# The scan's input in two PSUM banks, and seven other users in six: a decoder layer on one core

## The chip, the core and the metric

The kernel runs on one core of a Trainium2 chip. The metric is device time in microseconds: before the change 532.35 us, the median of 3 runs (530.22 to 536.63). The profile comes from one more execution, whose span is 528.4 us.

The core's engines run their own instruction streams and meet at semaphores: TensorE (PE; PEld is its weight load), VectorE (DVE), ScalarE (ACT), GpSimd (POOL) and SyncE (SP, which here issues DMAs). On-chip data lie in SBUF, or in PSUM, which has eight banks of 128 x 512 f32 that TensorE writes and that VectorE and ScalarE read and write.

## The reference

A decoder layer over 16 sequences of 128 tokens, width 128: a selective state-space scan with a mixture of 4 experts, attention to a context of 64 channels, and a second mixture of 8 experts with capacity. The change is in the first part:

```python
delta = jax.nn.softplus(jnp.einsum('bld,de->ble', x, Wd) + bd)
Bm = jnp.einsum('bld,ds->bls', x, WB) + bB
Cm = jnp.einsum('bld,ds->bls', x, WC) + bC
A = -jnp.exp(A_log)
def step(h, inps):
    x_t, d_t, B_t, C_t = inps
    bar_A = jnp.exp(jnp.minimum(d_t[:, :, None] * A, 2.0))
    bar_B = jnp.clip(d_t[:, :, None] * B_t[:, None, :], -2.0, 2.0)
    h = jnp.clip(bar_A * h + bar_B * x_t[:, :, None], -100.0, 100.0)
    y = jnp.sum(h * C_t[:, None, :], axis=-1) + x_t * D_param
    return (h, y)
...
hid = jax.nn.silu(jnp.einsum('nd,edf->enf', flat, up_w) + up_b[:, None, :])
all_out = jnp.einsum('enf,efd->end', hid, down_w) + down_b[:, None, :]
```

The state has 16 channels. The scan of one channel over time is one VectorE instruction on 128 x 512 elements (the model's width by four sequences).

## The kernel before, in words

**Tiles and units.** The 2048 tokens are four groups of 512 (`GW`). A unit is one state channel of one group: 64 units, 16 in a group. A loop over slots k, from -16 to past 64, is written out on every engine in the same order; slot k holds the work around unit k. A semaphore for each kind of result ties the streams. Nothing is scheduled at run time: each engine goes through its list in order, and a waiting instruction holds all behind it.

**One slot of the scan.** TensorE broadcasts a row B into bank 0 and a row C into bank 1 (`broadcast_row`, L1144). VectorE does `drive(k+1)` (L408: `bu = u * B`), `scan(k)` (L421: `h = a * h + bu` over time), `read_out(k-1)` (L456: `hc = h * C`) and then `around(k)`, a list of other work. GpSimd adds hc into yD (L871) when L456 is done. ScalarE makes the factors a by Exp, four units at once in each fourth slot (L970, `decay`), at least four slots ahead.

**TensorE's slot k** is `around(k)`, then `send_B(k+3)`, which waits until VectorE has read B of k+2, then `next_up(k+1)`, then `send_C(k+1)`, which waits until VectorE has done L456 of k. `up` (L1152) is one of the 16 up-projections of a group's mixture (4 experts by 4 tiles of 128); one is issued in a slot, from slot 16(g+1) on, so group g's mixture runs beside the scan of group g+1. ScalarE turns each into `hid` by a Silu (L983, `silu`), which is the last thing in its slot; TensorE's down-projections (L1161) read hid.

**The prologue** of group g+1 lies in the slots of group g's scan (that of group 0 ahead of all scans). Counted within a group's 16 slots: 2, turn xn (L1129) and copy it to xT on ScalarE (L961); 3, z = Wd x (L1172), B and C for all tokens (L1177), and on ScalarE Abs and Relu of z (L1029, L1032); 4, VectorE adds the bias to B and C and splits them in three bf16 parts (L356 to L366), ScalarE Exp and Ln; 5, transpose the parts (L1184) and copy them as `rows` (L1038); 6, the row of bounds (L1189), which VectorE reads in slot 12 (L375); 14, L1194, read in slot 15. Group 0's slots 7 to 14 also hold the transposes of fc1 (L1199), each copied out by ScalarE (L1045). The keys and values of attention are made in slots 10, 14 and 15 (`KV_SLOTS`).

**PSUM banks before:** 0 B, 1 C, 2 mixture (and z, keys, values), 3 and 4 up-projections in turn, 5 down-projections, 6 prologue, 7 attention. `claim(bank, reader)` makes TensorE wait for the last reader of the bank before it writes there again.

## Time and profile before

| what | before |
|---|---|
| median of 3 runs | 532.35 us (530.22 to 536.63) |
| span of the profiled execution | 528.4 us |
| PE, PEld busy | 342.2, 231.9 us |
| DVE busy | 354.0 us, 67% |
| ACT, POOL busy | 232.4, 225.2 us |
| the 64 scans L421 | 97.9 us busy, mean 1530 ns |
| the 64 adds L871 on POOL | 83.6 us busy, mean 1307 ns |
| DVE's waits for PE at L408 and L512 | 3.4 and 16.7 us |
| PE's waits for ACT at L1152 | 1.3 us in 2 places |

The page gives, for each line and kind of instruction, its busy time and the idle time of its engine just before it. A stretch of the timeline gives instructions in order of their start; brackets at a row's end hold how long its engine had been idle and what ended that. On TensorE one f32 product shows as two MATMUL rows merged to x2. The scan's loop lies between 25 and 302 us.

### The profile page before, as it was taken

What the parts mean: (1) busy time and instruction counts of PE and PEld (TensorE: products, weight loads), DVE (VectorE), ACT (ScalarE), POOL (GpSimd) and SP (SyncE); (2) the same over time, 40 slices, a digit from 0 to 9 for tenths busy, and PEclk for the clock granted to TensorE, in tenths of its full rate; (3) what the DMA queues carried; (4) which work ended last, traced back from release to release, by engine and by line L of the source; (5) the groups of instructions that cost most, each with busy time, mean ns of one, the idle gap of its engine ahead of it and who ended that gap; (6) DMA issues with size and microseconds to landing.
All of it is one profiled execution on the core that took longest, in us unless ns stands there. A gap on an engine that the chain in (4) does not pass through costs nothing.

```text
span 528.4 us, 5886 instructions
## 1 busy us (share of the span) xinstructions
PE 342.2 (65%) x1697; PEld 231.9 (44%) x1697; DVE 354.0 (67%) x977; ACT 232.4 (44%) x396; POOL 225.2 (43%) x214
## 2 busy tenths in 40 slices
PE   3216553859887769786795999873520799999200
PEld 2003231427544435463563667562310588898200
DVE  2579997996979999979999848557452012111085
ACT  2805533196643953575441385630200663553060
POOL 3313743436433345534334813342525035546354
PEclk9999999978989998989978999996555799999555
DMA  3999100000000000000000000010101311200152
GB/s 61 310 244 339 48 2 1 0 0 2 0 2 1 0 1 1 2 2 1 0 1 11 30 1 1 21 61 0 41 1 43 92 51 48 85 29 22 57 146 60
DMA packets 29464, 24.01 MB, mean 45 GB/s; under 512 B 5430, under 2 KB 23925, under 8 KB 29424
## 3 DMA queue, kind: packets, MB, share of 16 engines
q1 hardware_dynamic: 27032, 19.49, 13.4%
q0 software_dynamic: 2304, 4.04, 2.3%
q8 instruction: 14, 0.23, 0.2%
q14 instruction: 26, 0.21, 0.1%
q10 hardware_dynamic: 88, 0.03, 0.0%
HBM read 13.73 MB, written 10.52 MB: 46 GB/s over the span
## 4 chain that ended last, share of the span: by engine, by line
DVE 37%; PE 35%; issue 14%; ACT 5%; POOL 5%; DMA 3%; DVEq 1%; SPq 0%; ACTq 0%; POOLq 0%; another core or an unknown queue 0%
DVE h L421 9%; PE bank L1356 7%; PE bank L1345 6%; PE bank L1152 5%; PE bank L1161 5%; DVE hc L456 4%; PE bank L1144 3%; DVE stats L305 3%; DVE xrow L318 2%; DVE bu L408 2%; DVE acc L512 2%; DVE acc L328 2%; DVE mv L308 1%; DVE z L385 1%; DMA xT<-y_rows 1%
## 5 line engine op out<-in xcount | busy, mean ns | idle before, releaser
L871 POOL TENSOR_TENSOR yD<-yD,hc 128x512 f32<-128x512 f32 x64 | 83.6, 1307 | 138.4 <-DVE hc L456 118.5
L1144 PE MATMUL bank<-rows,selid 99*128 99x512 bf16 x128 | 61.7, 485 | 80.7 <-DVE bu L408 48.4
L421 DVE TENSOR_TENSOR_SCAN h<-a,bu 128x512 f32<-128x512 f32 x64 | 97.9, 1530 | 0.0
L1152 PE MATMUL bank<-yD,w 128*128 128x512 f32 x128 | 73.4, 658 | 1.7 <-ACT hid L983 1.3
L1161 PE MATMUL bank<-w,hid 128*128 128x128 f32 x512 | 73.3, 289 | 0.9 <-DVE lg L539 0.5
L1161 PEld LDWEIGHTS bank<-w,hid 128*128 128x128 f32 x512 | 67.2, 201 | 11.4 <-issue 8.9
L1144 PEld LDWEIGHTS bank<-rows,selid 99*128 99x128 bf16 x128 | 13.6, 108 | 132.5 <-DVE hc L456 70.6
L926 POOL DMA_INDIRECT y_rows<-yslot,dest x40 | 38.9, 973 | 52.5 <-DVE yslot L712 44.9
L712 DVE TENSOR_TENSOR yslot<-bank,w 128x128 f32<-128x128 f32 x40 | 11.6, 292 | 69.1 <-PE bank L1356 64.8
L983 ACT ACTIVATE hid<-bank,cols 128x512 f32<-128x512 f32 x64 | 43.7, 684 | 31.5 <-PE bank L1152 17.3
L408 DVE TENSOR_TENSOR bu<-u,bank 128x512 f32<-128x512 f32 x64 | 43.6, 682 | 18.7 <-issue 14.9
L1095 ACT ACTIVATE hid<-bank,cols 128x320 f32<-128x320 f32 x64 | 33.4, 527 | 29.5 <-PE bank L1345 25.5
L855 POOL TENSOR_TENSOR rstd<-vpe,nhalf 128x4 f32<-128x4 f32 x20 | 20.5, 1025 | 58.3 <-DVE vpe L310 57.9
L859 POOL DMA_INDIRECT slots_in<-xrow,posu x32 | 33.1, 1033 | 28.4 <-DVE ahead L585 18.1
L456 DVE TENSOR_TENSOR hc<-h,bank 128x512 f32<-128x512 f32 x64 | 42.1, 658 | 0.0
L970 ACT ACTIVATE a<-delta,A_sb 128x508 f32<-128x508 f32 x64 | 40.5, 706 | 0.0
L1356 PE MATMUL bank<-fc,hid 128*128 128x128 f32 x320 | 38.3, 279 | 2.8 <-DVE yslot L712 1.8
L1356 PEld LDWEIGHTS bank<-fc,hid 128*128 128x128 f32 x320 | 37.3, 195 | 3.3 <-DVE yslot L712 1.9
L1345 PE MATMUL bank<-w,fc1T 128*128 128x320 f32 x128 | 37.5, 447 | 1.7 <-ACT w L1085 1.7
L961 ACT ACTIVATE xT<-bank 128x512 f32<-128x512 f32 x12 | 7.2, 597 | 56.3 <-PE bank L1129 56.3
L1345 PEld LDWEIGHTS bank<-w,fc1T 128*128 128x128 f32 x128 | 24.6, 197 | 11.8 <-ACT w L1085 2.3
L512 DVE SCALAR_TENSOR_TENSOR acc<-bank,gate,acc 128x128 f32<-128x128 f32 x64 | 17.9, 341 | 16.7 <-PE bank L1161 16.7
(187 smaller groups left out, 536.0 us busy)
## 6 DMA issues: line engine op xcount, KB each, us to landing
slots_in<-yslot SPq DMA_DIRECT2D x10, 258.0 KB, 4.9
xe_tok<-slots_in SPq DMA_DIRECT2D x8, 322.5 KB
y_rows<-yslot SPq DMA_DIRECT2D x8, 256.0 KB, 4.5
x_tok<-in_x_dram SPq DMA_DIRECT2D x4, 256.0 KB, 5.2
w<-in_L_attn_up_w_dram SPq DMA_DIRECT2D x1, 1024.0 KB
yD<-y_rows SPq DMA_DIRECT2D x4, 256.0 KB, 4.3
xT<-y_rows SPq DMA_DIRECT2D x4, 256.0 KB, 5.6
out_dram<-acc SPq DMA_DIRECT2D x4, 256.0 KB, 2.3
```

What stands on the lines that cost most here:

```text
L408: do(v.tensor_tensor(bu[:, k % 2, :], grp(u, g), bank[B_BANK][:], ALU.mult))
L421: ins = v.tensor_tensor_scan(h[:, k % 2, :], a[:, k % A_RING, :, :].rearrange("p j n -> p (j n)"), bu[:, k % 2, :], 0.0, ALU.mult, ALU.add)
L456: do(v.tensor_tensor(hc[:, k % HC_RING, :], h[:, k % 2, :], bank[C_BANK][:], ALU.mult))
L871: pool.tensor_tensor(grp(yD, g), grp(yD, g), hc[:, k % HC_RING, :], ALU.add).then_inc(summed, 1)
L926: pool.indirect_dma_start(y_rows[:], bass.IndirectOffsetOnAxis(ap=dest[:, t // CT, t % CT:t % CT + 1], axis=0), yslot[:, q % 2, j * P:(j + ...
L970: act.activation(a[:, k % A_RING, :, 1:P], tiles3(grp(delta, g))[:, :, 1:P], ACT.Exp, scale=A_sb[:, s:s + 1]).then_inc(a_done, 1)
L983: act.activation(hid[:, m % 2, f, :], bank[UP_BANKS[f % 2]][:], ACT.Silu, bias=cols[:, C_UPB + i:C_UPB + i + 1]).then_inc(hid_done, 1)
L1144: pe.matmul(bank[b][:], selid[:, row:row + 1].to_broadcast([3 * NROW, P]), rows[:, g % 2, :], start=True, stop=True).then_inc(done, 1)
L1152: pe.matmul(bank[UP_BANKS[f % 2]][:], w1[:, e, f * P:(f + 1) * P], grp(yD, g), start=True, stop=True).then_inc(up_ps, 1)
L1161: ins = pe.matmul(bank[DOWN_BANK][:, j * P:(j + 1) * P], hid[:, m % 2, f, j * P:(j + 1) * P], w2[:, e, f, :], start=(f == 0), stop=(f == F ...
L1345: pe.matmul(bank[m % 4][:, 0:HALF], fc1T[:, e, f * P:(f + 1) * P], xeT[:, e % 2, hf * HALF:(hf + 1) * HALF], start=True, stop=True).then_i ...
L1356: ins = pe.matmul(bank[4 + t % 2][:, 0:P], hid2[:, e % 2, f, j * P:(j + 1) * P], fc2[:, e, f, :], start=(f == 0), stop=(f == FT - 1))
```

## The change

The scan's input bu leaves SBUF for banks 2 and 3 of PSUM, which units use in turn. L408 now writes there, L421 reads there. The mixture's bank and the prologue's bank become one, bank 4. Up-projections have bank 5 alone, down-projections bank 6. Only the last group, whose mixture comes after the last scan, still has two banks for its up-projections: 5, and bank 0, where B was. The bound row L1189 moves from slot 6 to slot 11, keys and values from slots 14 and 15 to 12 and 13, and the counts of the last two groups move from the prologue's bank to bank 1.

```diff
-KV_SLOTS = [[NS * (g + 1) + r for r in (10, 14, 15)] for g in range(G - 2)]
+KV_SLOTS = [[NS * (g + 1) + r for r in (10, 12, 13)] for g in range(G - 2)]
...
-        B_BANK, C_BANK, MIX_BANK, DOWN_BANK, PRE_BANK, ATT_BANK = 0, 1, 2, 5, 6, 7
-        UP_BANKS = (3, 4)
+        B_BANK, C_BANK, MIX_BANK, UP_BANK, DOWN_BANK, ATT_BANK = 0, 1, 4, 5, 6, 7
+        PRE_BANK = MIX_BANK
+        BU_BANKS = (2, 3)
...
+        def drive_of(k):
+            return bank[BU_BANKS[k % 2]][:]
+        def up_bank(g, f):
+            return UP_BANK if g < G - 1 or f % 2 == 0 else B_BANK
...
-                do(v.tensor_tensor(bu[:, k % 2, :], grp(u, g), bank[B_BANK][:], ALU.mult))
+                do(v.tensor_tensor(drive_of(k), grp(u, g), bank[B_BANK][:], ALU.mult))
...
-                                               bu[:, k % 2, :], 0.0, ALU.mult, ALU.add)
+                                               drive_of(k), 0.0, ALU.mult, ALU.add)
...
-                if m >= 2:
-                    pe.wait_ge(hid_done, m - 1)
+                if g < G - 1:
+                    if m:
+                        pe.wait_ge(hid_done, m)
+                else:
+                    pe.wait_ge(hid_done, m if i == 0 else m - 1)
+                    pe.wait_ge(dve_done, at["b", UNITS - 1])
...
-                if (g := pre_at(k, 6)) is not None:
+                if (g := pre_at(k, 11)) is not None:
                     o = claim(PRE_BANK, (dve_done, at["bmax", g]))
```

Two places on TensorE. The first is the prologue of group 0; L1172 and L1183 are z, L1177 and L1188 are B and C for all tokens, names in brackets are semaphores waited for. Before:

```order
L1172 MATMUL bank2<-xT,wd_sb 128x512 [waits xT_done0,ld_w]
L1177 MATMUL bank6<-wbc_sb,xT 128x32 [waits xT_done0]
L1177 MATMUL bank6<-wbc_sb,xT 128x32 x3
L1184 MATMUL bank6<-ident_bf,parts 99x128 [waits dve_done]
L1184 MATMUL bank6<-ident_bf,parts 99x128 x3
```

After:

```order
L1183 MATMUL bank4<-xT,wd_sb 128x512 [waits xT_done0,ld_w]
L1188 MATMUL bank4<-wbc_sb,xT 128x32 [waits relu_done]
L1188 MATMUL bank4<-wbc_sb,xT 128x32 x3
L1195 MATMUL bank4<-ident_bf,parts 99x128 [waits dve_done]
L1195 MATMUL bank4<-ident_bf,parts 99x128 x3
```

B and C now go to the bank in which z lies, and wait until ScalarE's Relu has read z. The same pair stands in slots 3, 19 and 35.

The second place is slots 19 to 21, in the middle of group 0's mixture; bank0 and bank1 are B and C, w1 is the up-projection's weight. Before:

```order
L1152 MATMUL bank4<-yD,w1 128x512 [waits hid_done]
L1144 MATMUL bank1<-rows,selid 128x512 [waits rows_done,dve_done]
L1144 MATMUL bank0<-rows,selid 128x512 [waits rows_done,dve_done]
L1152 MATMUL bank3<-yD,w1 128x512 [waits hid_done]
L1144 MATMUL bank1<-rows,selid 128x512 [waits rows_done,dve_done]
L1184 MATMUL bank6<-ident_bf,parts 99x128 [waits dve_done]
L1184 MATMUL bank6<-ident_bf,parts 99x128 x3
L1144 MATMUL bank0<-rows,selid 128x512 [waits rows_done,dve_done]
L1152 MATMUL bank4<-yD,w1 128x512 [waits hid_done]
```

After:

```order
L1163 MATMUL bank5<-yD,w1 128x512 [waits hid_done]
L1151 MATMUL bank1<-rows,selid 128x512 [waits rows_done,dve_done]
L1151 MATMUL bank0<-rows,selid 128x512 [waits rows_done,dve_done]
L1163 MATMUL bank5<-yD,w1 128x512 [waits hid_done]
L1151 MATMUL bank1<-rows,selid 128x512 [waits rows_done,dve_done]
L1195 MATMUL bank4<-ident_bf,parts 99x128 [waits dve_done]
L1195 MATMUL bank4<-ident_bf,parts 99x128 x3
L1151 MATMUL bank0<-rows,selid 128x512 [waits rows_done,dve_done]
L1163 MATMUL bank5<-yD,w1 128x512 [waits hid_done]
```

The order is the same. What moved is the count that `hid_done` is waited for: each up-projection now waits for the Silu of the one before it, not of the one before that, and the next row C stands behind it.

## Rows read from the trace of the kernel before

**Rows 1.** The page: the span and each engine's busy time.
```profile
span 528.4 us, 5886 instructions
PE 342.2 (65%) x1697; PEld 231.9 (44%) x1697; DVE 354.0 (67%) x977; ACT 232.4 (44%) x396; POOL 225.2 (43%) x214
```

**Rows 2.** Groups by line and form: count, busy us, mean ns, idle before.
```profile
L421 DVE TENSOR_TENSOR_SCAN h<-a,bu 128x512 f32<-128x512 f32 x64 | 97.9, 1530 | 0.0
...
L456 DVE TENSOR_TENSOR hc<-h,bank 128x512 f32<-128x512 f32 x64 | 42.1, 658 | 0.0
...
L712 DVE TENSOR_TENSOR yslot<-bank,w 128x128 f32<-128x128 f32 x40 | 11.6, 292 | 69.1 <-PE bank L1356 64.8 <-issue 4.2
...
L734 DVE TENSOR_TENSOR acc<-acc,yD 128x512 f32<-128x512 f32 x3 | 2.1, 687 | 0.0
```

**Rows 3.** Stretches by group, L421 alone: length, DVE busy us (count), clock, DMA, GB/s.
```profile
29.00:89.00 60.00, 28.76 (x16) 1.00 0.45 133
89.00:155.00 66.00, 23.36 (x16) 0.87 0.00 1
155.00:228.00 73.00, 22.40 (x16) 0.98 0.00 1
228.00:301.00 73.00, 23.38 (x16) 0.88 0.02 6
```

**Rows 4.** Timeline, group 0: start us, length us, engine, line, operation.
```profile
49.38 1.22 DVE L421 TENSOR_TENSOR_SCAN h<-a,bu 128x512 f32<-128x512 f32 x1
...
57.46 1.27 POOL L871 TENSOR_TENSOR yD<-yD,hc 128x512 f32<-128x512 f32 x1 [1.80 <-DVE hc L456]
...
57.84 1.97 DVE L421 TENSOR_TENSOR_SCAN h<-a,bu 128x512 f32<-128x512 f32 x1
...
62.07 2.19 POOL L889 TENSOR_TENSOR u<-delta,xT 128x512 f32<-128x512 f32 x1
63.12 0.66 DVE L456 TENSOR_TENSOR hc<-h,bank 128x512 f32<-128x512 f32 x1
```

**Rows 5.** Timeline: prologue of group 0, then of group 1 (last row).
```profile
11.38 1.75 PE L1177 MATMUL bank<-wbc_sb,xT 128*128 128x32 f32 x8
...
12.21 0.68 ACT L1032 ACTIVATE delta<-bank,cols 128x512 f32<-128x512 f32 x1
...
13.37 0.29 DVE L356 TENSOR_TENSOR bcm<-bank,bbc_b 128x128 f32<-128x128 f32 x1 [5.57 <-PE bank L1177]
...
46.74 0.29 DVE L356 TENSOR_TENSOR bcm<-bank,bbc_b 128x128 f32<-128x128 f32 x1 [0.89 <-PE bank L1177]
```

**Rows 6.** Timeline, slot 8: ScalarE between two copies of fc1.
```profile
59.49 1.28 ACT L970 ACT_TABLE_LOAD   x1
...
63.24 0.57 ACT L1045 ACTIVATE fc1T<-bank 128x512 f32<-128x512 f32 x1
```

**Rows 7.** Timeline, slots 20 and 21: Silu 3 (115.43) and what TensorE does.
```profile
111.23 1.02 PE L1152 MATMUL bank<-yD,w 128*128 128x512 f32 x2
...
115.43 0.69 ACT L983 ACTIVATE hid<-bank,cols 128x512 f32<-128x512 f32 x1
...
116.00 0.66 DVE L456 TENSOR_TENSOR hc<-h,bank 128x512 f32<-128x512 f32 x1
...
116.17 2.07 PE L1152 MATMUL bank<-yD,w 128*128 128x512 f32 x2 [0.55 <-ACT hid L983]
```

**Rows 8.** Timeline, slots 24 and 25: up-projection 8, Silu 7, L456 of unit 25.
```profile
128.26 1.02 PE L1152 MATMUL bank<-yD,w 128*128 128x512 f32 x2
...
129.83 0.69 ACT L983 ACTIVATE hid<-bank,cols 128x512 f32<-128x512 f32 x1
...
130.20 0.66 DVE L456 TENSOR_TENSOR hc<-h,bank 128x512 f32<-128x512 f32 x1
```

**Rows 9.** Timeline, slot 48: up-projection 32 and Silu 31.
```profile
232.64 1.02 PE L1152 MATMUL bank<-yD,w 128*128 128x512 f32 x2
...
233.53 0.69 ACT L983 ACTIVATE hid<-bank,cols 128x512 f32<-128x512 f32 x1
```

More of the change, by code:

```diff
@@ L138, in decoder_layer @@
         a = sb("a", [P, A_RING, GT, P])
-        bu = sb("bu", [P, 2, GW])
         h = sb("h", [P, 2, GW])
@@ L282, in count_bank @@
         def count_bank(g):
-            return ATT_BANK if g < G - 2 else PRE_BANK
+            return ATT_BANK if g < G - 2 else C_BANK
+        def drive_of(k):
+            return bank[BU_BANKS[k % 2]][:]
+        def up_bank(g, f):
+            return UP_BANK if g < G - 1 or f % 2 == 0 else B_BANK
         def tiles3(t):
@@ L429, in scan_clipped @@
                 hk = tiles3(h[:, k % 2, :])
-                bk_ = tiles3(bu[:, k % 2, :])
+                bk_ = tiles3(drive_of(k))
                 ak = a[:, k % A_RING, :, :]
@@ L436, in step @@
                     v.sem_clear(slow_done)
-                bk2 = bu[:, k % 2, :]
+                bk2 = drive_of(k)
                 hk2 = h[:, k % 2, :]
@@ L982, in silu @@
                     act.wait_ge(dn_ps, GT * (m - 1))
-                act.activation(hid[:, m % 2, f, :], bank[UP_BANKS[f % 2]][:], ACT.Silu,
+                act.activation(hid[:, m % 2, f, :], bank[up_bank(g, f)][:], ACT.Silu,
                                bias=cols[:, C_UPB + i:C_UPB + i + 1]).then_inc(hid_done, 1)
@@ L1114, in _ @@
             pe.transpose(bank[ATT_BANK][:, 0:NVEC], vecs[:], ident[0:NVEC, 0:NVEC]).then_inc(cols_ps, 1)
-            read = {MIX_BANK: None, PRE_BANK: None, ATT_BANK: (cols_done, 1)}
+            read = {MIX_BANK: None, C_BANK: (dve_done, at["hc", UNITS - 1]), ATT_BANK: (cols_done, 1)}
             def claim(b, reader):
@@ L1149, in up @@
                 m = (g * E1 + e) * FT + f
-                if m >= 2:
-                    pe.wait_ge(hid_done, m - 1)
-                pe.matmul(bank[UP_BANKS[f % 2]][:], w1[:, e, f * P:(f + 1) * P], grp(yD, g),
+                if g < G - 1:
[4 more added lines that the diff above has]
+                    pe.wait_ge(dve_done, at["b", UNITS - 1])
+                pe.matmul(bank[up_bank(g, f)][:], w1[:, e, f * P:(f + 1) * P], grp(yD, g),
                           start=True, stop=True).then_inc(up_ps, 1)
@@ L1330, in turn_expert @@
                     claim(MIX_BANK, None)
-                    claim(PRE_BANK, None)
+                    claim(C_BANK, None)
                     claim(ATT_BANK, None)
```

## The prediction

> **What bounds the kernel now.** I read the page first: VectorE is busy 354.0 of 528.4 us, TensorE 342.2 [rows 1], so neither bounds the whole. The activity by slices does: from 25 to 302 us VectorE stands at seven to nine tenths, so the scan's loop is VectorE's; behind it TensorE takes over, and the change leaves that part nearly as it is. The reader then looks for what VectorE does in the loop that isn't work. The costliest group is the scan L421, 97.9 us in 64 pieces, mean 1530 ns [rows 2]. A scan that nothing disturbs takes 1.22 us, and the one at 57.84 takes 1.97: its excess of 0.75 is the time until GpSimd's add L871, begun at 57.46 for 1.27 us, is over [rows 4]. So a scan and a GpSimd operation exclude each other here. The whole excess is 97.9 - 64 x 1.215 = 20.1 us; by group, 28.76 - 16 x 1.215 = 9.3, and in the same way 3.9, 3.0 and 3.9 [rows 3].
>
> L456, which reads h from SBUF and the other operand from PSUM, isn't disturbed: at 63.12, inside L889's 2.19 us, it takes its 0.66 [rows 4]. That is what makes the change work. The Trainium skill (SBUF — State Buffer, Who interferes with whom) says that a VectorE instruction with two SBUF inputs contends with GpSimd's reads and one with at most one doesn't; both rows agree.
>
> **What the change takes away.** All 20.1 us of excess, if nothing else is late. In group 0 VectorE is the only bound, and there empty slots should shrink from 3.07 to 2.31 us. (3.07 is what lies between the starts of scans 7 and 8; 0.76 of it is excess.) L871 gets no longer, so GpSimd, 225.2 us busy [rows 1], isn't the next bound.
>
> **What reading and writing PSUM costs.** No row here shows VectorE writing a large tile to PSUM, nor a scan that reads it. The nearest: a product with a PSUM operand takes 658 ns, and the sum of two SBUF operands 687 [rows 2], so reading costs nothing that shows, and I take 0. The bound above comes from the fixed part of an instruction: 128 elements take 292 ns and 512 take 658 [rows 2], 0.95 ns an element, which leaves 170 ns. If half of that came again for each of two instructions, it would be 64 x 2 x 85 = 10.9 us at most; I keep 4 of it for the range, since reading, one of the two sides, shows none. The Trainium skill (Perfetto Trace Analysis, Optimizing Scalar/DVE Operations) speaks against 0: it puts a VectorE instruction's access at about 60 ns in SBUF and about 125 in PSUM. By it the estimate would be 64 x 2 x 65 ns = 8.3 us on top of the sum below.
>
> **What sharing the prologue's bank costs.** B and C for all tokens (L1177) begin at 11.38, when z's first reader hasn't started; now they wait until Relu has read z, which ends at 12.21 + 0.68 = 12.89 [rows 5]. That is 1.5 us, in full on the path at the start, because VectorE stands waiting for L1177 at 13.37 [rows 5]. In slot 3 of group 0 it waits there again, 0.89 us at 46.74 [rows 5]: the two shorter scans ahead (2 x 0.76) buy nothing, as TensorE comes only one of them earlier, and 1.5 - 0.76 = 0.8 is added. Give-back: 1.5 + 0.8 = 2.3 us. In slots 19 and 35 the same wait costs 0.7 us beyond the shorter scan, but it lies ahead of the larger stall below and vanishes in it. The bound row, keys and values wait for each other's readers too; their readers come within a slot, and I cost them in the stall of slots 28 and 44 alone.
>
> **What a faster VectorE meets in group 0.** ScalarE's batch of four decays takes it from 59.49 to 63.24, and then it copies fc1 out for 0.57 [rows 6]. TensorE's next transposes wait for that copy, and the row B of slot 11 stands behind them. At 3.07 us a slot this was just in time; at 2.31 the row comes 1.3 us late. Group 0 nets -9.3 + 2.3 + 1.3 = -5.7.
>
> **What one bank for the up-projections costs.** This is the large term. In TensorE's slot k the up-projection now waits for the last instruction of ScalarE's slot k, and row C of unit k+1 stands behind it, for which VectorE's L456 waits. In each fourth slot ScalarE has the four decays with two table loads before that Silu, and in slots 20 and 36 the prologue's Exp and Ln with two more.
>
> Slot 20: up-projection 4 ran at 111.23; Silu 3 ends at 115.43 + 0.69 = 116.12 [rows 7]. It waits 4.9 us. Up-projection 5 waited for that same Silu before, and took 2.07 us at the lower clock, where 1.02 is usual [rows 7]. So row C starts near 118.1 and ends near 118.5, and L456 wanted it at 116.00 [rows 7]: 2.5 us late. Then up-projection 5 must wait for Silu 4, which ScalarE can only do after it has copied the rows out that TensorE transposes behind row C; that adds 1.1. Shift 3.6 us.
>
> Slot 24: up-projection 8 ran at 128.26, Silu 7 ends at 130.52 [rows 8], 2.3 us late; L456 at 130.20 [rows 8] needs the row C behind, at 131.9. TensorE works without a gap until 133, so the whole 2.3 arrives, and up-projections 9 and 10 add some tenths each: 3.3 us less what the shorter scan 28 wins in that stretch, so 2.5.
>
> Slots 28 to 31: the wait is 2.2 us plus 0.7 for the key copy, which now precedes the Silu; the downs and values behind it run late at a low clock. I work out that the end of group 1 comes 1 us later here instead of 1.1 sooner by its other two scans. Sum for group 1: 3.6 + 2.5 + 1 = +7, as against -3.9. If TensorE is fast in the stalls (1 us less for each up-projection there) and VectorE's other work covers some, it is +3; if the shifts add up in full, +9.
>
> Group 2: slot 36 repeats slot 20 (4.9 us of wait), but TensorE's clock is high there and VectorE has more of its own to do: +2.4. Slot 44 repeats slot 28 (3.8 us) : +1.6 after its scans' 2.2 are spent. Together +4, bounds +1 and +6. Group 3: slot 48, up-projection 32 at 232.64 against Silu 31's end at 234.22 [rows 9], 1.6 us late with TensorE full behind it; the gains of its scans (two at the start, two at the end) are all in slots where row C is now late. +1.5, bounds -2 and +3. In all, six up-projections wait 1.6 to 4.9 us; the other 42 wait 1 us or less, mostly nothing.
>
> **The sum.** Start +1.5; group 0: -9.3, with 0.8 + 1.5 for the two scans that buy nothing and 1.3 for the copy, -5.7; group 1 +7; group 2 +4; group 3 +1.5; PSUM 0; the tail, where the last group keeps two banks, 0. That is +8.3 on the profiled 528.4, so 536.7. The span stands 4 us under the median of the runs; the same shift on the median gives 532.35 + 8.3, about 540.5.
>
> **Rivals.**
> - *The exclusion is all that matters.* The Silu is never late, since VectorE's slots leave room. Then group 0's 5.7 and two thirds of the other groups' 10.8 stay: 1.5 - 5.7 - 7 = -11, 521. For it: TensorE waited for a Silu in 2 places only, 1.3 us. Against: that was with a bank in reserve, and the six gaps are read off directly. It decides from where ScalarE's batch fits into one slot of VectorE's; in slot 20 it is 4.9 us too long. Faster. Chance 0.1.
> - *The stalls half cancel*: VectorE's other work covers them and the clock stays high. 1.5 - 5.7 + 3 + 1 - 1 = -1, 531. Chance 0.25.
> - *The forecast*, 535 to 543. Chance 0.3.
> - *The stalls add up, and TensorE slows in each.* An up-projection costs 2.07 instead of 1.02 and the downs behind it double: 1.5 - 5 + 9 + 6 + 3 = +14.5, 547. Chance 0.2.
> - *Access to PSUM is dear.* The forecast and between 4 and 10.9 us: 544 to 551. Chance 0.1. The Trainium skill's rule (same page as above) is this case, and its estimate would be 532.35 + 8.3 + 8.3 = 549.
> - *PSUM cures nothing*: a scan that reads its input there still waits for GpSimd. The 20.1 us stay and the give-backs come on top, 1.5 + 0.8 + 1.3 + 11 + 7 + 5.5 = 27, 559. L456's row speaks against it. Chance 0.05.
>
> **Range and chances.** 527 to 551 holds the second to the fifth case, 0.85 less some of their edges. A measurement tells 2% from no change, 10.6 us: below 521.7 faster, above 543 slower. The first case gives 0.1 for faster; the last three 0.35 for slower; the rest is 0.55.
>
> **What would show it.** The scans' mean at 1.21 to 1.25 us (above that PSUM cures less or is dearer); empty slots of group 0 at 2.3; TensorE's waits for a Silu at L1163 up from 1.3 us to some 15, and waits of VectorE for row C ahead of its product with it, of which there are none now; the wait for B and C of all tokens up from 6.5 to about 11 us. If VectorE waits for no row C, the large term is wrong and the first rival holds. If the end of group 0 isn't some 4 us earlier, my account of its slots is wrong.

## The result and the profile after

The changed kernel is slower: 560.6 us (553.7 to 561.8, 4 runs) against 532.8 for the kernel before, ratio 1.051 [1.046, 1.056]. Run again later, on one of the chips of the experiments (e14), it takes 550.5 against 526.4, ratio 1.045 [1.040, 1.049]. The forecast was 540.5 and the range ended at 551. Medians here and below take in every run, while the ratios leave out runs more than 1.5% above the fastest of their kernel (two of the four of e11 and one of the four of e2). The recorded ratios also differ from the quotients of the medians by up to 0.4% where nothing is left out.

The page and the groups of the changed kernel, in answer to [rows 1, 2]; L428, L415, L463, L1163 and L1172 are what L421, L408, L456, L1152 and L1161 were.

```profile
span 560.1 us, 5902 instructions
...
PE 371.0 (66%) x1697; PEld 247.7 (44%) x1697; DVE 336.6 (60%) x977; ACT 233.7 (42%) x396; POOL 218.9 (39%) x214
...
L1163 PE MATMUL bank<-yD,w 128*128 128x512 f32 x128 | 85.3, 754 | 27.6 <-ACT hid L990 27.2
...
L1172 PE MATMUL bank<-w,hid 128*128 128x128 f32 x512 | 82.3, 314 | 0.0
L428 DVE TENSOR_TENSOR_SCAN h<-a,bank 128x512 f32<-128x512 f32 x64 | 77.6, 1212 | 0.0
...
L415 DVE TENSOR_TENSOR bank<-u,bank 128x512 f32<-128x512 f32 x64 | 44.3, 691 | 23.8 <-issue 14.9 <-PE bank L1151 8.4
...
L463 DVE TENSOR_TENSOR hc<-h,bank 128x512 f32<-128x512 f32 x64 | 42.5, 664 | 14.7 <-issue 13.2 <-DVE h L428 1.4
...
L519 DVE SCALAR_TENSOR_TENSOR acc<-bank,gate,acc 128x128 f32<-128x128 f32 x64 | 18.0, 344 | 38.8 <-PE bank L1172 38.8
```

VectorE has 17.4 us less work and the profiled execution takes 31.7 us longer. (It is the slowest of the changed kernel's four; the medians are 27.7 apart.) The scan fell from 1530 to 1212 ns: the 20 us of excess are gone. In their place stand waits: VectorE's product with row C (L463), which waited for nothing before, waits 14.7 us (the page calls most of it "issue"; each piece ends when a row C lands), the sum of the experts (L519) waits 38.8 us for the down-projections, where the kernel before had 16.7, and TensorE waits 27.2 us for a Silu, where it had 1.3. TensorE's work also got longer with nothing added to it: the up-projections' mean is 754 ns and was 658.

Where the time goes, stretch by stretch, from the start of the scans 0, 16, 32, 48 and 63 in both kernels. The changed kernel's rows:

```profile
34.35 1.21 DVE L428 TENSOR_TENSOR_SCAN h<-a,bank 128x512 f32<-128x512 f32 x1
...
88.81 1.21 DVE L428 TENSOR_TENSOR_SCAN h<-a,bank 128x512 f32<-128x512 f32 x1
...
166.85 1.21 DVE L428 TENSOR_TENSOR_SCAN h<-a,bank 128x512 f32<-128x512 f32 x1
...
252.14 1.21 DVE L428 TENSOR_TENSOR_SCAN h<-a,bank 128x512 f32<-128x512 f32 x1
...
320.51 1.21 DVE L428 TENSOR_TENSOR_SCAN h<-a,bank 128x512 f32<-128x512 f32 x1
```

The kernel before starts the same scans at 30.46, 90.54, 156.16, 228.62 and 297.66. The last column is the profile of the later run, e14 (span 549.8). Both columns are differences to the one profile of the kernel before, span 528.4; on the chips of the experiments that kernel is faster and was not profiled. So the last column sums to 21.4, where the medians differ by 24.2.

| stretch | forecast | measured | second profile |
|---|---|---|---|
| start, to scan 0 | +1.5 | +3.9 | +3.4 |
| group 0 | -5.7 | -5.6 | -5.6 |
| group 1 | +7 | +12.4 | +10.1 |
| group 2 | +4 | +12.8 | +10.5 |
| group 3 | +1.5 | -0.7 | -0.1 |
| tail | 0 | +8.8 | +3.2 |
| sum | +8.3 | +31.7 | +21.4 |

From here on slot k means the time between the starts of scans k and k+1. A stall that the forecast put into TensorE's slot k shows there in slot k+2 or thereabouts: its slots 20, 24, 28, 36 and 44 are 22, 26, 30, 38 and 46 below.

**One of the stalls in group 1.** TensorE's timeline of the changed kernel in slots 26 and 27, then VectorE's: start us, length us, and in brackets the idle time ahead and what ended it.

```profile
132.37 1.12 PE L1163 MATMUL bank<-yD,w 128*128 128x512 f32 x2 [1.74 <-ACT hid L990]
133.33 0.38 PE L1151 MATMUL bank<-rows,selid 99*128 99x512 bf16 x1
...
135.65 2.08 PE L1172 MATMUL bank<-w,hid 128*128 128x128 f32 x8
137.51 0.63 PE L1151 MATMUL bank<-rows,selid 99*128 99x512 bf16 x1
138.56 2.08 PE L1163 MATMUL bank<-yD,w 128*128 128x512 f32 x2 [0.41 <-ACT hid L990]
140.43 0.63 PE L1151 MATMUL bank<-rows,selid 99*128 99x512 bf16 x1
```

```profile
133.81 0.69 DVE L463 TENSOR_TENSOR hc<-h,bank 128x512 f32<-128x512 f32 x1 [1.32 <-issue]
137.76 1.13 DVE L519 SCALAR_TENSOR_TENSOR acc<-bank,gate,acc 128x128 f32<-128x128 f32 x4 [3.26 <-PE bank L1172]
...
144.09 0.70 DVE L415 TENSOR_TENSOR bank<-u,bank 128x512 f32<-128x512 f32 x1 [2.24 <-PE bank L1151]
```

TensorE waits 1.74 us for a Silu, row C lands 1.3 us late (133.81), and that was nearly the forecast's whole account. But the down-projections behind it are late as well, they take 2.08 us at the lower clock where 1.06 is usual, VectorE's sum of the experts stands 3.26 us for them, and in the next slot a row B is 2.24 us late. Slots 26 and 27 are 3.5 and 3.0 us longer than in the kernel before.

**The largest one,** slot 46 in group 2: TensorE of the changed kernel, v is L1274 and the scores are L1287.

```profile
236.50 1.82 PE L1163 MATMUL bank<-yD,w 128*128 128x512 f32 x2 [3.05 <-ACT hid L990]
238.11 0.63 PE L1151 MATMUL bank<-rows,selid 99*128 99x512 bf16 x1
238.68 2.07 PE L1274 MATMUL bank<-wv_sb,ctxT 64*128 64x128 f32 x8
240.68 2.07 PE L1287 MATMUL bank<-delta,yD 128*128 128x128 f32 x8
242.55 1.57 PE L1172 MATMUL bank<-w,hid 128*128 128x128 f32 x8
```

VectorE gets row C 2.58 us late, then waits 4.63 us for these down-projections, and the slot is 7.0 us longer. The kernel before, scores, downs, and v two slots later:

```profile
215.86 1.06 PE L1276 MATMUL bank<-delta,yD 128*128 128x128 f32 x8
216.75 1.06 PE L1161 MATMUL bank<-w,hid 128*128 128x128 f32 x8
...
224.60 1.16 PE L1263 MATMUL bank<-wv_sb,ctxT 64*128 64x128 f32 x8
```

The lower clock alone is 0.8 + 0.9 + 1.0 + 0.5 = 3.2 of the 7 (1.82, 2.07, 2.07 and 1.57 against 1.02, 1.16, 1.06 and 1.06).

### The profile page after: what moved, and what is told of

It reads as the page before. It is cut to its first block, busy times and chain, and to the rows that moved or that the text cites. A ratio compares the mean times of both kernels' runs of the same rounds, so it can differ in the third digit from the quotient of the medians.

```text
span 560.1 us, 5902 instructions
## 1 busy us (share of the span) xinstructions
PE 371.0 (66%) x1697; PEld 247.7 (44%) x1697; DVE 336.6 (60%) x977; ACT 233.7 (42%) x396; POOL 218.9 (39%) x214
## 4 chain that ended last, share of the span: by engine, by line
PE 44%; DVE 25%; ACT 15%; issue 9%; DMA 3%; POOL 2%; another core or an unknown queue 1%; DVEq 1%; SPq 0%; ACTq 0%; POOLq 0%
PE bank L1163 9%; PE bank L1172 7%; PE bank L1367 6%; PE bank L1356 6%; DVE h L428 4%; PE bank L1151 4%; ACT hid L990 3%; ACT a L977 3%; DVE stats L312 2%; DVE hc L463 2%; DVE xrow L325 2%; DVE acc L335 2%; ACT L990 2%; DVE bank L415 1%; PE bank L1136 1%
## 5 line engine op out<-in xcount | busy, mean ns | idle before, releaser
L1163 PE MATMUL bank<-yD,w 128*128 128x512 f32 x128 | 85.3, 754 | 27.6 <-ACT hid L990 27.2
L1151 PE MATMUL bank<-rows,selid 99*128 99x512 bf16 x128 | 64.9, 512 | 49.7 <-DVE bank L415 36.7
L1172 PE MATMUL bank<-w,hid 128*128 128x128 f32 x512 | 82.3, 314 | 0.0
L1172 PEld LDWEIGHTS bank<-w,hid 128*128 128x128 f32 x512 | 76.6, 226 | 11.3 <-issue 9.6
L428 DVE TENSOR_TENSOR_SCAN h<-a,bank 128x512 f32<-128x512 f32 x64 | 77.6, 1212 | 0.0
L415 DVE TENSOR_TENSOR bank<-u,bank 128x512 f32<-128x512 f32 x64 | 44.3, 691 | 23.8 <-issue 14.9
L1151 PEld LDWEIGHTS bank<-rows,selid 99*128 99x128 bf16 x128 | 14.5, 115 | 91.8 <-DVE bank L415 47.3
L463 DVE TENSOR_TENSOR hc<-h,bank 128x512 f32<-128x512 f32 x64 | 42.5, 664 | 14.7 <-issue 13.2
L1102 ACT ACTIVATE hid<-bank,cols 128x320 f32<-128x320 f32 x64 | 33.7, 527 | 28.2 <-PE bank L1356 23.6
L1163 PEld LDWEIGHTS bank<-yD,w 128*128 128x128 f32 x128 | 25.4, 228 | 40.3 <-ACT hid L990 33.5
L866 POOL DMA_INDIRECT slots_in<-xrow,posu x32 | 31.7, 990 | 28.4 <-DVE ahead L592 18.1
L519 DVE SCALAR_TENSOR_TENSOR acc<-bank,gate,acc 128x128 f32<-128x128 f32 x64 | 18.0, 344 | 38.8 <-PE bank L1172 38.8
L1367 PE MATMUL bank<-fc,hid 128*128 128x128 f32 x320 | 37.1, 275 | 1.5 <-issue 1.5
```

The source lines that it names most:

```text
L415: do(v.tensor_tensor(drive_of(k), grp(u, g), bank[B_BANK][:], ALU.mult))
L428: ins = v.tensor_tensor_scan(h[:, k % 2, :], a[:, k % A_RING, :, :].rearrange("p j n -> p (j n)"), drive_of(k), 0.0, ALU.mult, ALU.add)
L463: do(v.tensor_tensor(hc[:, k % HC_RING, :], h[:, k % 2, :], bank[C_BANK][:], ALU.mult))
L1151: pe.matmul(bank[b][:], selid[:, row:row + 1].to_broadcast([3 * NROW, P]), rows[:, g % 2, :], start=True, stop=True).then_inc(done, 1)
L1163: pe.matmul(bank[up_bank(g, f)][:], w1[:, e, f * P:(f + 1) * P], grp(yD, g), start=True, stop=True).then_inc(up_ps, 1)
L1172: ins = pe.matmul(bank[DOWN_BANK][:, j * P:(j + 1) * P], hid[:, m % 2, f, j * P:(j + 1) * P], w2[:, e, f, :], start=(f == 0), stop=(f == F ...
```

## The experiments

Four sets, each with its own runs of the kernel before. The record numbers a different chip for each (8, 10, 3 and 0), which isn't what the expectation of e14 says; the kernel before took 526.8, 526.5, 526.4 and 526.3 us in them, so times of different sets are compared here as they stand. Ratios are to the kernel before of the same set. The sets are e1 to e4; e5, e10, e9, e11; e12 to e15; e18, e17, e16. There is one profile of each kernel, of one execution, which is the kernel's fastest for e1, e2, e10, e11, e17 and e18 and its slowest for e5, e12 and e15.

| kernel | us | ratio [95%] |
|---|---|---|
| e1 new banks, bu in SBUF | 563.8 | 1.073 [1.069, 1.076] |
| e2 one up-projection bank only | 562.1 | 1.071 [1.066, 1.077] |
| e3 shared bank only | 534.9 | 1.015 [1.010, 1.019] |
| e4 one bank for bu, two for up | 524.8 | 0.996 [0.994, 0.998] |
| e5 changed, Silu first | 547.0 | 1.037 [1.033, 1.040] |
| e10 changed, B and C apart | 551.3 | 1.046 [1.044, 1.049] |
| e9 bu over row B | 525.4 | 0.998 [0.994, 1.001] |
| e11 e2 and extra products | 553.6 | 1.041 [1.037, 1.044] |
| e12 bu in PSUM in group 0 alone | 517.9 | 0.982 [0.980, 0.985] |
| e14 the changed kernel | 550.5 | 1.045 [1.040, 1.049] |
| e13 e5 and e10 | 536.6 | 1.021 [1.017, 1.025] |
| e15 e9, half the downs | 529.4 | 1.006 [1.004, 1.009] |
| e18 changed, tail's banks swapped | 550.6 | 1.046 [1.043, 1.050] |
| e17 all three mends | 527.3 | 1.001 [0.996, 1.005] |
| e16 e9, rows B twice | 529.6 | 1.006 [1.003, 1.009] |

**Which part of the change costs.** e1 takes the changed kernel and puts bu back:

```diff
         def drive_of(k):
-            return bank[BU_BANKS[k % 2]][:]
+            return bu[:, k % 2, :]
```

> The changed kernel with the scan's input bu put back into SBUF, in the new banks. Theory P (the loss lies in the banks that bu took from the others): the scans' excess returns, 64 x (1.53 - 1.21) = 20 us, of which group 0's shift of 9 us must show in full and the rest partly, since VectorE waits in groups 1 to 3: 566 to 578 us. Rival Q (bu in PSUM itself costs something, for instance in TensorE's or ScalarE's access to the other banks): 532 to 545, with the waits for the Silu gone.

e2 takes the kernel before and changes the up-projections' bank alone:

```diff
+        def up_bank(g, f):
+            return bank[UP_BANKS[0 if g < G - 1 else f % 2]]
...
-                if m >= 2:
-                    pe.wait_ge(hid_done, m - 1)
+                if g < G - 1:
+                    if m:
+                        pe.wait_ge(hid_done, m)
+                else:
+                    pe.wait_ge(hid_done, m if i == 0 else m - 1)
```

> The kernel before with one thing changed: one bank for the up-projections of groups 0 to 2 (the last group keeps two). Theory P1 (the single up-projection bank is the loss): 555 to 568 us, groups 1 and 2 lose together 20 us or more, and TensorE waits for a Silu in some 20 places. Rival P2 (the bank shared by prologue and mixture is the loss): 533 to 540. By the forecast's own terms, 7 + 4 + 1.5 plus the scans' gain of 3.9 + 3.0 + 3.9 in groups 1 to 3 that these are net of, 23 in all: 555.

e3 takes the kernel before with `PRE_BANK = MIX_BANK`, the bound row in slot 11 and keys and values in slots 12 and 13:

> The kernel before with one thing changed: prologue and mixture share a bank, with the bound row in slot 11 and keys and values in slots 12 and 13. Theory P1: the start costs 3.9 us (the wait for the Relu, and the casts of B and C that now fall beside GpSimd's two products), slots 3, 19 and 35 together some 2 more: 535 to 540 us. Rival P2: 550 to 565.

The up-projections' one bank alone costs 35.3 us, the shared bank 8.1, both together without the gain 37.0 (2 us less than the expectation's lower end), and with bu in PSUM 24.2. So the gain is there, 12.8 of the 20 us, and rival Q, by which bu in PSUM itself was the cost, falls. In the profiles of e1 and e14 7.4 of it come in group 0 and 3.5 in groups 1 to 3, where the excess was 10.8. e2's profile has the same waits as the changed kernel's, 40.8 us for a Silu in 26 places. e3's last scan is 8.4 us late, with 4.0 at the start, 1.7 in slot 4, 1.5 in slot 20 and 2.8 in slot 42, and some given back elsewhere.

**Two up-projection banks beside PSUM.** e4 gives bu one bank, so that the product for the next scan must come after the scan (and row B is sent one slot later, which the lines leave out):

```diff
-                if 0 <= k + 1 < UNITS and k >= 0:
-                    drive(k + 1)
                 if 0 <= k < UNITS:
                     scan(k, clipped)
                 if 1 <= k <= UNITS:
                     read_out(k - 1)
+                if 0 <= k + 1 < UNITS and k >= 0:
+                    drive(k + 1)
```

> The scan's input in one PSUM bank in place of two, so that the up-projections keep two; VectorE's slot is scan, read-out, then the product for the next scan, and row B is sent one slot later. Prologue and mixture still share a bank. Theory P1: the scans stay at 1.21, the waits for the Silu fall to some 2 us, the start keeps its 3.9, group 0 gains 6, groups 1 to 3 gain up to 10: 519 to 526 us. Rival P2: 545 to 560, since the shared bank stays. Rival R (the product's new place makes the next scan wait for it in each empty slot, or row B comes late): 0.1 to 0.5 us in each of some 40 slots, so 525 to 540.

524.8: the Silu's waits are gone (2.5 us under the scan), but the gain is 2 us, where 8 were possible by the expectation. Each empty slot takes 2.44 us in place of 2.31, and VectorE waits 18.6 us for rows B in groups 1 to 3. e9 shall have neither fault: row B alternates between two banks and the product is written over it. It also reads unit k out in slot k, so that row C is wanted a slot sooner, and moves B and C for all tokens to the attention's bank.

```diff
+        B_BANKS = (0, 2)
         def drive_of(k):
-            return bank[BU_BANKS[k % 2]][:]
+            return bank[B_BANKS[k % 2]][:]
...
                 if 0 <= k < UNITS:
                     scan(k, clipped)
-                if 1 <= k <= UNITS:
-                    read_out(k - 1)
+                if 0 <= k + 1 < UNITS and k >= 0:
+                    drive(k + 1)
+                if 0 <= k < UNITS:
+                    read_out(k)
```

> All gains and neither loss: row B has two banks in turn and VectorE's product u*B is written over the row in its own bank, where the scan reads it, so that two up-projection banks remain; the slot on VectorE is scan k, product k+1, read-out k; B and C for all tokens in the attention's bank. If the losses are the one up-projection bank and the shared prologue bank alone, then before less 20.3 for the scans, plus 1.3 for the copy of fc1: 508 to 512 where before takes 526.8. Rival R, as in the kernel with one bank for bu: each scan or read-out waits some tenths for the instruction before it: 515 to 525. Rival T (TensorE's row B, C and up-projection become the bound at 2.3 us a slot): 515 to 525 with VectorE waiting for rows B or C.

525.4, above both rivals' ranges. e9 is 8.7 us ahead at scan 16 and has lost all of it by scan 63 (297.64 against 297.66), though its scans take 1213 to 1216 ns in every group. VectorE waits for rows B and C instead, 19.3 us in 25 places. So in these two kernels a shorter scan in groups 1 to 3 is worth nothing, and TensorE, which serves rows, up- and down-projections in order, is what VectorE waits for. That no kernel could have that part of the gain isn't shown: both also ask for their rows at other times than the kernel before, and no run separates that from the shorter scan.

**The start and the order on ScalarE.** e10 keeps B and C for all tokens and their transposed rows in the attention's bank (one of four places that change is shown):

```diff
-                    o = claim(PRE_BANK, (dve_done, at["bc", g]))
+                    o = claim(ATT_BANK, (dve_done, at["bc", g]))
```

> The changed kernel with B and C for all tokens and their transposed rows in the attention's bank, which is free in those slots, so that they no longer wait for the Relu. Theory: the start gives back its 3.9 us, slot 4 to 5 its 1.7; the stall of slot 20, which comes from the Silu, stays, and so does all from there on: 6 us less than the changed kernel, 547.5 where before takes 526.8. Rival: the gain at the start is swallowed by the stalls behind it, as TensorE and not VectorE sets them: under 2 us less.

Against the profile of e14 it starts scan 0 4.0 us sooner and is 6.7 us ahead at scan 16, but only 2.2 at scan 63, and the median is no better (551.3 against 550.5). The rival holds: with one up-projection bank the stalls behind, in slots 38, 50 and 54, take the lead back. Behind e5's mend the same move is worth 10.4 us (547.0 to 536.6, below), so the losses don't add. e5 moves the `silu` loop to the top of ScalarE's slot:

> The changed kernel with one move on ScalarE: the Silu of a slot stands first in the slot, ahead of the four decays, the copies and the Exp and Ln, in place of last. Theory P1 in the form of the forecast (the Silu is late because the decays stand ahead of it): most of the one-bank loss goes, 560 on the first chip becomes 535 to 545, or on a chip where before takes 526.8, 529 to 539; TensorE's waits for the Silu fall from 27 to under 10 us. Rival S (the chain is serial for another reason: the Silu waits for the downs, the up-projection for the Silu, row C for the up-projection, whatever ScalarE does beside it): within 5 us of the changed kernel, 548 to 558 where before takes 526.8.

3.5 us less than the changed kernel, within rival S's 5 us of it and far from P1's 529 to 539: by itself the order on ScalarE is a small part of the loss. At the last scan it is 7.3 us ahead, and in the tail, where the early Silu stands waiting for the downs, it loses 3.1. TensorE still waits 22.7 us for a Silu, in 11 places in place of 23 (e14: 28.2), where under 10 were expected; what fell are VectorE's waits behind it, for the downs from 15.9 to 5.0 us and for row C from 9.5 to 4.2, between 85 and 305 us. Both mends:

> The changed kernel with both mends: the Silu first in ScalarE's slot, and B and C for all tokens in the attention's bank. If the two losses are separate and each mend gives what it gave alone at the last scan (11.9 and 6.8 us): 18.7 less than the changed kernel, 535 where before takes 526.8. If TensorE's rows and downs are what bounds groups 1 to 3 behind them: some 10 less, 543.

536.6, and at the last scan 1.7 us ahead of the kernel before. What is left of the loss lies behind it: from scan 63 to the end 239.5 us, where the kernel before has 230.7 and e12, below, 227.5.

**The changed kernel again.**

> The changed kernel as it is, on the same chip as the other runs, so that they can be compared without a ratio over two chips. From the ratio 1.0507: 553.5 where before takes 526.8; a second profile shows whether the stalls stand in the same slots (22, 26, 27, 30, 38, 46) or move with TensorE's clock. If the stalls are set by the program alone: the same slots within 0.3 us. If the clock has a part: the same slots with up to 2 us more or less in each.

The large stalls are in the same slots. Up to slot 21 the two profiles agree within 0.6 us; then they part where TensorE's clock does, up to 2.2 us in a slot (+0.78 against -1.38 in slot 23), and 4.6 us in all by scan 63. TensorE in slot 23, in the first profile and then in e14:

```profile
118.59 2.08 PE L1163 MATMUL bank<-yD,w 128*128 128x512 f32 x2 [0.84 <-ACT hid L990]
...
120.89 1.92 PE L1172 MATMUL bank<-w,hid 128*128 128x128 f32 x8
```

```profile
118.10 1.12 PE L1163 MATMUL bank<-yD,w 128*128 128x512 f32 x2 [0.86 <-ACT hid L990]
...
119.28 1.05 PE L1172 MATMUL bank<-w,hid 128*128 128x128 f32 x8
```

The program and the wait are the same, and the granted clock of the slot and the one before it is 0.50 and 0.74.

**The tail.** The last group's first up-projection waits for the last Silu of the group before, `m if i == 0`, as both use bank 5. In the changed kernel that Silu stands behind the attention's Exps and two table loads:

```profile
327.67 1.28 ACT L1010 ACT_TABLE_LOAD   x1
...
330.49 1.28 ACT L990 ACT_TABLE_LOAD   x1
331.79 0.69 ACT L990 ACTIVATE hid<-bank,cols 128x512 f32<-128x512 f32 x1
...
332.73 2.05 PE L1163 MATMUL bank<-yD,w 128*128 128x512 f32 x2 [3.00 <-ACT hid L990]
...
337.58 0.61 DVE L519 SCALAR_TENSOR_TENSOR acc<-bank,gate,acc 128x128 f32<-128x128 f32 x2 [11.45 <-PE bank L1172]
```

e18 lets the last group start in row B's old bank:

```diff
-            return UP_BANK if g < G - 1 or f % 2 == 0 else B_BANK
+            return UP_BANK if g < G - 1 or f % 2 else B_BANK
...
-                    pe.wait_ge(hid_done, m if i == 0 else m - 1)
+                    pe.wait_ge(hid_done, m - 1)
```

> The changed kernel, in which the last group's up-projections start in the bank of row B in place of the single up-projection bank, so that the first of them needn't wait for the last Silu of the group before. If that wait is what makes the tail longer: the first sum of the last group's experts comes 5.5 us sooner after the last scan (at +11.6 as in the kernel before, in place of +17 to +18), and the time is 5 us less than the changed kernel's 550.5, ratio to before 1.035. Rival (the tail is late because the decays, Exps and table loads of ScalarE are, and the up-projection only shows it): within 1.5 us of the changed kernel.

The wait of L519 is back at what the kernel before has there (6.87 us):

```profile
331.28 1.13 DVE L519 SCALAR_TENSOR_TENSOR acc<-bank,gate,acc 128x128 f32<-128x128 f32 x4 [6.87 <-PE bank L1172]
```

From scan 63 to the end it takes 227.7 us in the profile, against 233.9 in e14. The fitting yardstick is e12 of the same set as e14, whose code behind scan 63 is that of the kernel before and which takes 227.5; the profile of the kernel before has 230.7, with stalls that e12 doesn't have, one of them here, first before and then e12:

```profile
347.73 1.13 DVE L528 SCALAR_TENSOR_TENSOR x_tok<-bank,rps,x_tok 128x128 f32<-128x128 f32 x4 [3.54 <-issue]
```

```profile
341.98 1.12 DVE L531 SCALAR_TENSOR_TENSOR x_tok<-bank,rps,x_tok 128x128 f32<-128x128 f32 x4 [1.25 <-issue]
```

So the wait for the last Silu makes the tail of e14 some 6 us longer and not 3.2, and e18 takes all of it away in the profile. The median didn't move, 550.6 against 550.5 (profiled were the fastest of e18's six runs and one in the upper half of e14's): the mechanism is shown, its worth in the whole is not. With all three mends, and the Silu first only up to slot 63:

> The changed kernel with the Silu first in ScalarE's slot up to slot 63 and last behind it, B and C for all tokens in the attention's bank, and the swap of the last group's banks. The kernel with the first two mends had its last scan 1.7 us ahead of before but a tail 9 us longer, since there the early Silu stood waiting for the down-projections. If the tail is as before's again: 525 to 528 where before takes 526.4, so that all of the change's loss is accounted for by the three waits. If the tail stays long: 533 to 537.

527.3 (522.6 to 530.4, 6 runs), level with the kernel before: the three mends together take away 23 of the change's 24 us, while alone they gave 3.5, nothing and nothing. How the 23 divide among them is therefore not defined by these runs. One bank still costs something here, as much as the PSUM gain is worth: TensorE still waits 20.9 us for a Silu, in 12 places.

**The clock.** e11 is e2 with work added where TensorE would stand:

```diff
+                    if i in (4, 8, 12):
+                        for _ in range(6):
+                            pe.matmul(bank[4][:], selid[:, 0:1].to_broadcast([3 * NROW, P]), rows[:, g % 2, :],
+                                      start=True, stop=True)
                     if m:
                         pe.wait_ge(hid_done, m)
```

> The kernel with only the one up-projection bank changed (562.1 on this base), with six extra products of 128x512 into the free bank, which nobody reads, ahead of up-projections 4, 8 and 12 of each group, where TensorE would stand and wait for the Silu. Theory C (half of the loss is TensorE's lower clock behind each wait): the granted clock from 145 to 205 us rises from 0.74 towards 0.9, up-projections and downs behind the waits run at 1.0 us instead of 2.1, and the time falls by 8 us or more, to 545 to 554. Rival (the serial chain is the loss, the clock hardly): 558 to 568.

The stretch from 145 to 205 us in e2, then in e11: length, PE, PEld, DVE, ACT, POOL busy (count), granted clock, DMA, GB/s.

```profile
145.00:205.00 60.00, 45.43 (x173) 28.25 (x173) 43.46 (x101) 27.93 (x40) 19.23 (x15) 0.74 0.00 1
```

```profile
145.00:205.00 60.00, 43.37 (x200) 25.07 (x198) 50.94 (x110) 34.91 (x49) 22.29 (x19) 0.93 0.00 1
```

The granted clock rises from 0.74 to 0.93, up-projections take 663 ns in the mean instead of 733, and 54 products that nobody needs make the program 8.5 us faster by the medians. The runs scatter: e11 took 547.5, 548.8, 558.3 and 559.4 us, e2 558.1, 562.0, 562.3 and 567.1. So TensorE's clock is a quarter of the one bank's 35 us by the medians and two fifths by the ratios (1.041 against 1.071), net of what the extra products cost. e15 goes the other way, e9 with two of each four products of the downs left out:

```diff
-                for f in range(FT):
+                for f in range(0, FT, 3):
                     ins = pe.matmul(bank[DOWN_BANK][:, j * P:(j + 1) * P], hid[:, m % 2, f, j * P:(j + 1) * P],
```

> The kernel with bu over row B, with half of the first mixture's down-projection left out (two of four products of each block), which takes some 38 us of TensorE's work away, most of it under the scan. Theory T (with the scans at 1.21 us TensorE bounds groups 1 to 3, which is why this kernel gains nothing there): VectorE's waits for rows B and C fall from 20 us to under 5, and the time falls by 12 us or more, to 513 or less where before takes 526.8. Rival (order and latency on VectorE and ScalarE eat the gain): 521 to 526.

It is not faster but 4 us slower. From 85 to 265 us, e9 and then e15:

```profile
85.00:265.00 180.00, 137.98 (x624) 89.18 (x622) 148.69 (x330) 98.02 (x143) 71.27 (x57) 0.84 0.00 1
```

```profile
85.00:265.00 180.00, 137.27 (x469) 79.07 (x468) 142.22 (x318) 95.70 (x140) 67.58 (x54) 0.73 0.00 1
```

A quarter of the records less, at a clock of 0.73 instead of 0.84, and TensorE is as busy as before; the up-projections went from 685 to 776 ns. VectorE's waits for rows B and C between 85 and 305 us, which theory T had fall under 5 us, are 20.7 (e9: 19.3). Theory T in the form "too much work on TensorE" falls. What is left is how fast TensorE answers; that its clock is a large part of it is suggested and not measured. e16 gives e9 more work, the broadcast of row B twice in 48 slots:

> The kernel with bu written over row B, in which TensorE sends each row B of groups 1 to 3 twice, one product of 128x512 more in each of 48 slots. Theory C (TensorE's clock, which falls with too little work, costs more than work does): the granted clock from 85 to 265 us rises from 0.81 to 0.90 towards 0.95, and the time stays within 2 us of 525.4 or falls, though TensorE does some 20 us more work. Rival (TensorE's work is the bound in these slots): the time rises by 8 us or more, to 533 and above.

4.2 us slower, the granted clock from 85 to 265 us at 0.84 as in e9. Neither side is met: here the extra work didn't raise the clock, and it cost a fifth of its some 21 us.

**A version that beats both.** In group 0 no mixture runs, so the up-projections' banks are free and the exclusion is dearest there. e12 is the kernel before with

```diff
+        def drive_of(k):
+            return bank[UP_BANKS[k % 2]][:] if k < NS else bu[:, k % 2, :]
```

in place of bu, in its fallback path too.

> The kernel before with bu in PSUM for units 0 to 15 only, in the two up-projection banks, which nothing uses before the first mixture; from unit 16 on bu is in SBUF as before. No other bank changes hands. Theory (only group 0's excess is worth anything, and it carries over whole to the end): -9.3 for its scans, +1.3 for the copy of fc1 that TensorE then waits for, -8.0: 518.8 where before takes 526.8, ratio 0.985. Rival (TensorE sets the pace of group 1 and eats it): within 2 us of before.

517.9 (515.9 to 523.4, 7 runs), ratio 0.982 [0.980, 0.985]: 8.5 us faster than before, clear of noise though under 2%, and 33 faster than the changed kernel. In its profile, that of the slowest run, scan 16 starts 7.8 us sooner; the lead is 6.3 at scan 32, 6.1 at 48 and 3.5 at 63.

## Why the prediction was wrong

The forecast was +8.3 us and the profile shows +31.7. Two steps failed. The large term, what one bank for the up-projections costs, was priced in groups 1 and 2 by the row C behind each late up-projection, and took little of the down-projections behind it and of the clock they meet: +11 against +25.2. And the tail was put at 0, which overlooked a wait: +8.8. The start gave 2.4 more than forecast. The direction, the removal of the excess and the places of the waits were right.

**PSUM (right).** Forecast: scans at 1.21 to 1.25 us and access at nothing. Measured 1212 ns, L415 at 691 where L408 was at 682, L463 at 664 against 658. "PSUM cures nothing" and "access is dear" fall; the Trainium skill's 60 against 125 ns (Perfetto Trace Analysis, Optimizing Scalar/DVE Operations) would have made the scan and its product 65 ns longer each; the scan isn't longer and the product is by 9. Its rule on who interferes with whom (the Trainium skill, SBUF — State Buffer, Who interferes with whom) holds in e1, e2 and e3: 1519 to 1542 ns with bu in SBUF, against 1212.

**Group 0 (right).** -5.7 forecast, -5.6 measured. The copy of fc1 cost 1.0 of the 1.3 forecast, in the slot foreseen. The forecast's own sign, the end of group 0 some 4 us earlier, came out at 1.7 (88.81 against 90.54), because the start took back the rest.

**The start (mis-sized, +1.5 against +3.9).** Only the wait for the Relu was counted. VectorE's first reader of B and C, L363, comes at 15.12 instead of 13.37, as forecast, and so its successors fall beside GpSimd's first products:

```profile
15.45 1.26 POOL L892 TENSOR_TENSOR delta<-delta,z 128x512 f32<-128x512 f32 x1 [9.07 <-ACT z L1023]
...
16.79 1.26 POOL L896 TENSOR_TENSOR u<-delta,xT 128x512 f32<-128x512 f32 x1
```

```profile
15.70 1.10 DVE L369 CAST parts<-bcm 128x132 bf16<-128x132 f32 x1
16.83 1.37 DVE L370 TENSOR_TENSOR rem<-bcm,parts 128x132 f32<-128x132 f32 x1
```

They took 0.23 and 0.30 us in the kernel before, in group 0. The exclusion that the change removes from the scans came back in another pair. The Trainium skill says that a cast can take the shared ports too (SBUF — State Buffer, Who interferes with whom); the trace agrees, with 1.10 us for the cast beside L892, and I applied the rule to the scan alone. VectorE's waits for B and C for all tokens are 14.5 us in the four groups, where about 11 were forecast.

**Group 1 (mis-sized, +7 against +12.4).** "Slot 20" was forecast at 3.6 and gave 2.95 + 0.78 = 3.7 in slots 22 and 23. That this fits is in part luck: in e14, where up-projection 5 ran at the upper clock, the two slots give 1.6. The term that failed is "slot 24: 2.5", which gave 6.6 in slots 24 to 27, and "slots 28 to 31: +1", which gave 2.1: together 8.7 against 3.5. The gaps between up-projection and Silu were read rightly, but each was priced by the one row C behind it. The downs behind it are late too, VectorE's L519 waits for them (3.26 and, in slot 30, 2.82 us), the next Silu waits for them as well, and TensorE runs at the lower clock behind most of the long waits, if not at once then some products later (a granted clock of 0.50 in slots 22 and 23, downs of 2.08 us in slot 26). The waits themselves were read nearly right: five of the six are there with 1.7 to 4.5 us, 15 in all, the sixth (up-projection 32) is 0.6, and no other is above 1 us before the last scan. The cost wasn't in the up-projections' waits but in what stood behind.

**Group 2 (mis-sized, +4 against +12.8).** "Slot 36, clock is high there, +2.4" gave 6.4 in slots 34 to 39 (e14: 4.6), most of it in slot 38:

```profile
195.97 2.08 PE L1163 MATMUL bank<-yD,w 128*128 128x512 f32 x2 [2.90 <-ACT hid L990]
...
198.56 0.69 DVE L463 TENSOR_TENSOR hc<-h,bank 128x512 f32<-128x512 f32 x1 [2.65 <-issue]
```

The clock was high in the kernel before, 1.00 from 171 to 192 us, and 0.86 in the same slots of the changed one (184 to 209). I took the clock from the kernel before as if it belonged to the slot. "Slot 44 repeats slot 28, +1.6" gave 6.5 net in slots 42 to 47: the values, moved two slots ahead, stand between row C and the downs, which the forecast had only in "slots 28 to 31". e2, which doesn't move them, loses 1.4 in slot 46, and e3, which moves them but keeps two up-projection banks, nothing; e1 and the changed kernel, which do both, lose 5.2 and 7.0. So it is the two together. Why e2 in turn loses 5 us each in slots 38, 50 and 58, of which the changed kernel has only the first, wasn't settled.

**The tail (wrong, 0 against +8.8 and +3.2).** "The last group keeps two banks" overlooked the wait of its first up-projection, which is in the diff. The first sum of the last group's experts comes 5.5 us later after scan 63 (+17.1 against +11.6), and in e14 the tail is 6.5 us longer than that of e12. e1 and e2, which have the wait too, have tails of 230.9 and 231.4 us beside 226.9 of e3 in the same set. The rest of the 8.8 in the first profile are stalls behind it whose cause stays open.

**The rival that came nearest** was "the stalls add up, and TensorE slows in each", +14.5 with its +9 and +6: the mechanism that the runs show, at a chance of 0.2, with the additions to start and tail left out and group 2 still at half its size. The forecast gave the reverse case, half cancelling, more.

## What to carry over

A buffer taken from a pair is costed along the whole chain behind the wait: each product that stands behind the waiting one on its engine, who waits for it, and each of them at the lower clock as well. A loss that is measured alone may vanish beside a larger one, and show once that is gone. Ask for each stretch which engine is next in line: in these kernels a gain on VectorE was worth its full size only in the group in which TensorE had little to do, and there it could be had without taking a bank from anybody. A resource that lies idle in one phase (two banks in group 0) can be lent for that phase alone.

## What the runs showed of the hardware

- TensorE with half of a product's work left out made the program slower (e15, 529.4 against 525.4) at a granted clock of 0.73 against 0.84; idle time filled with useless products made another faster (e11, medians 553.6 against 562.1) at 0.93 against 0.74 from 145 to 205 us. The same up-projection takes 1.02 us at the upper level (2.4 GHz) and 2.08 at the lower (1.2 GHz).
- Two profiles of the same changed kernel differ by 10.3 us (560.1 and 549.8), nearly all behind slot 21, where TensorE's waits begin; 5.7 of it lie behind scan 63. A profile's span is a poor measure of a difference of 5 us here; e18 shows a gain in it that the median doesn't.
- VectorE may write a product over the PSUM operand it reads (e9, 678 ns; into another bank 691, into SBUF 682).
